# A four-layer graph network on one core: the last 68 gathered groups of the fourth layer summed from the gather's buffers, and a bias moved to GpSimd

## The reference

```python
# first layer: an MLP on each node's features and its summed edge features
agg = segment_sum(edge_attr, senders, N)
h = relu(concatenate([agg, nodes], axis=1) @ W1 + b1)      # 256 -> 512
return h @ W2 + b2                                         # 512 -> 128: b2 is the bias that moves

# second and third layer: sums of neighbours' rows x[src], dense matrices (no part of the change)

# fourth layer: attention with three heads; row2, col2 are the edges' starts and ends
a_src = einsum('nhc,hc->nh', (x @ W).reshape(n, 3, 128), att_src)     # a_dst alike
alpha = leaky_relu(a_src[row2] + a_dst[col2] + a_edge)
m = segment_max(alpha, col2, n)
ex = exp(alpha - m[col2])
attn = ex / segment_sum(ex, col2, n)[col2]
agg = segment_sum(attn[:, :, None] * xp[row2], col2, n)
y = (agg.reshape(n, 384) + gat_bias) @ lin_W + lin_b
```

## Time and profile before

| | us |
|---|---|
| median of 3 runs (lowest, highest) | 3746.25 (3742.75, 3749.92) |
| the profiled execution, its own time | 3734.14 |
| its span, first to last instruction | 3732.5 |
| PE busy over the span | 2576.2 (69%) |
| DVE busy | 1566.4 (42%) |
| POOL busy | 1376.2 (37%) |
| ACT busy | 705.3 (19%) |
| mean granted clock of PE | 0.768 |

### The profile page before, as it was taken

The page is one execution under the profiler, slowest core; times in us unless marked ns, Lnnn a source line. Parts: engine busy times, 40 slices in busy tenths (PEclk is TensorE's granted clock), DMA queues, the critical chain, the costliest instruction groups (busy, mean ns, idle before and its releaser), DMA issues. The chain is left out here.

```text
span 3732.5 us, 72094 instructions
## 1 busy us (share of the span) xinstructions
PE 2576.2 (69%) x21824; PEld 2171.2 (58%) x21825; DVE 1566.4 (42%) x3762; ACT 705.3 (19%) x1093; POOL 1376.2 (37%) x1473
## 2 busy tenths in 40 slices
PE   1699999897999459996998155545550156566675
PEld 0566666784888348885887144444440156565564
DVE  5466666123111631112333455554568233233367
ACT  0287777252000410001000000000000100000033
POOL 4222222111000212221444655555530566666545
PEclk9899999897999669998999555555565555555577
DMA  4388888423887178886998555555540466666621
GB/s 119 106 282 280 283 283 283 145 58 119 283 282 248 50 221 251 247 250 194 290 291 244 139 126 124 130 131 123 128 99 13 129 171 180 170 177 173 172 67 42
DMA packets 597630, 662.89 MB, mean 178 GB/s; under 512 B 268059, under 2 KB 449388, under 8 KB 596905
## 3 DMA queue, kind: packets, MB, share of 16 engines
q1 hardware_dynamic: 276921, 405.43, 35.2%
q10 hardware_dynamic: 270440, 182.02, 17.5%
q0 software_dynamic: 50208, 74.70, 8.3%
HBM read 502.38 MB, written 159.93 MB: 177 GB/s over the span
## 5 line engine op out<-in xcount | busy, mean ns | idle before, releaser
L866 POOL DMA_INDIRECT rows<-x_rows,src_i x832 | 813.9, 978 | 663.7 <-issue 228.4
L1500 PE MATMUL ps<-slices,wide 128*128 128x250 f16 x7350 | 829.0, 271 | 55.8 <-DVE wide L2168 34.1
L1500 PEld LDWEIGHTS ps<-slices,wide 128*128 128x128 f16 x7350 | 716.3, 98 | 143.9 <-DVE wide L2168 50.3
L1450 PE MATMUL ps<-weighted,slices 128*128 128x57 f32 x1664 | 386.8, 421 | 324.8 <-issue 155.6
L1726 PE MATMUL ps<-slices 128*128 128x75 bf16 x4992 | 366.8, 249 | 332.1 <-issue 288.8
L1450 PEld LDWEIGHTS ps<-weighted,slices 128*128 128x128 f32 x1664 | 365.1, 329 | 346.4 <-issue 201.0
L1726 PEld LDWEIGHTS ps<-slices 128*128 x4992 | 309.4, 130 | 389.4 <-issue 387.7
L906 POOL TENSOR_TENSOR ea_one<-ea,ones 128x64 f32<-128x64 f32 x250 | 137.3, 550 | 454.5 <-DMA ea<-in_edge_attr 435.0
L1395 PE MATMUL ps<-rows,weighted 128*32 128x128 f32 x2000 | 272.1, 280 | 14.4 <-DMA ea<-in_edge_attr 11.8
L1395 PEld LDWEIGHTS ps<-rows,weighted 128*32 128x32 f32 x2000 | 202.4, 111 | 59.5 <-issue 51.5
L2468 DVE TENSOR_TENSOR hT<-ps,hT 128x600 f32<-128x600 f32 x104 | 81.1, 781 | 326.3 <-remote 161.9
(11 more groups left out here) (354 smaller groups left out, 3356.7 us busy)
## 6 DMA issues: line engine op xcount, KB each, us to landing
slices<-adjacency SPq DMA_DIRECT2D x525, 437.5 KB, 4.4
rows<-in_edge_attr SPq DMA_DIRECT2D x250, 256.0 KB
x_of_edges<-rows SPq DMA_DIRECT2D x208, 256.0 KB
slices<-x_of_edges ACTq DMA_DIRECT2D x208, 256.0 KB
adjacency<-wide ACTq DMA_DIRECT2D x91, 437.5 KB, 3.1
adjacency<-slices ACTq DMA_DIRECT2D x84, 437.5 KB, 3.1
slices<-src_low ACTq DMA_DIRECT2D x52, 512.0 KB
rows<-x_rows,src_i POOLq DMA_INDIRECT x832
```

The costliest lines, as they stand in the source:

```text
L866: pool.indirect_dma_start(out=packed[i][:, c, :], out_offset=None, in_=table, in_offset=bass.IndirectOffsetOnAxis(ap=rows_of, axis=0)).the ...
L1450: mm = pe.matmul(ps_a[i][:, width * h:width * (h + 1)], rows3[i][:, n, :], weighted[:, i, n, :, :].rearrange("p h w -> p (h w)"), start=(c ...
L1500: mm = pe.matmul(ps_d[b], high_low[:, part, QS * s + q, :], slices[:, s, PN * q:PN * (q + 1)], start=(s == 0 and q == 0 and part == 0), st ...
```

## The change

In the fourth layer the last 68 groups (FRESH; groups 140 to 207) are neither stored nor loaded back: PE multiplies straight from `packed`, the gather's own buffers. The first 140 (STORED) go the old way. The order of summing changes: four stored groups, then 17 rounds of 12 positions; each third position of a round is a fresh group, so that a round takes 8 stored and 4 fresh ones. PE's loop has 12 groups a turn instead of 4, DVE's too, ACT's too. Offsets are loaded to registers 8, and then 16 + 8 a round. POOL waits for scoring passes up to g = 113 instead of 103, no more for `scan_done`, and no more for a number of summed groups ahead of group 144; from there it waits until the fresh group four before has been summed. SP's loop of stores has 35 turns of four in place of 52.

In the first layer the fifth matmul of each tile goes, two in a pair. The bias is loaded to all 125 partitions, POOL adds it in place to the residual rows xb when they have landed, one pair ahead of its stores, and DVE waits for that (`x_shifted`) where it waited for the load.

```diff
-                if g >= RING:
+                if RING <= g < STORED + RING:
                     pool.wait_ge(xe_stored[i], 16 * (g // RING))
-                if SCORES_LEAD <= g < SCANNED_AT:
+                if g >= STORED + RING:
+                    pool.wait_ge(group_summed, SUMMED + place(0, 3 * (g - RING - STORED) + 2) + 1)
+                if SCORES_LEAD <= g < SCORES_LEAD + PASSES:
                     pool.wait_ge(scores_begun, g - SCORES_LEAD + 1)
-                if g == SCANNED_AT:
-                    pool.wait_ge(scan_done, 1)
-                if g >= SCANNED_AT + SUMS_LEAD:
-                    pool.wait_ge(group_summed, SUMMED + 2 * (g - SCANNED_AT - SUMS_LEAD) + 1)
...
+            def refill(u, last):                                        # ACT
+                for j in range(MIX):
...
+                    act.wait_ge(group_summed, SUMMED + place(u, j) + 1)
+                    if not is_fresh(j) and not (last and n >= RING):
+                        load_stored(RING + 2 * RING * u + n + RING, 2 + 2 * u + n // RING, n % RING)
+                    load_att(summed_group(u, j + RING), j % RING)
...
+                with pe.Fori(0, MIXED) as u:                            # PE
+                    for j in range(MIX):
+                        n = stored_at(j)
+                        if is_fresh(j):
+                            group(place(u, j), j % RING, packed[j // 3], fetched(j // 3, u))
+                        else:
+                            group(place(u, j), j % RING, rows3[n % RING], arrived(n % RING, 1 + 2 * u + n // RING))
...
-                with v.Fori(0, NIT // 2 - 1) as k:                      # DVE
-                    two_iterations(k, False)
+                def mixed(u, last):
+                    stored = bases_of(regs[0:2 * AH], RING + 2 * RING * u, 2 * RING)
+                    fresh = bases_of(regs[2 * AH:3 * AH], STORED + RING * u, RING)
+                    for j in range(MIX):
+                        p = place(u, j)
+                        if not (last and j + LEAD >= MIX):
+                            make(summed_group(u, j + LEAD), (j + LEAD) % RING)
+                        if not (last and j + 2 >= MIX):
+                            weights(p + 2, 1 + 3 * u + (j + 2) // RING, (j + 2) % RING)
+                        add(p, j % RING, fresh[j // 3] if is_fresh(j) else stored[stored_at(j)])
...
+            def biased0(q, u, s):                                       # POOL, first layer
+
+                pool.wait_ge(*d0.landed(s, u))
+                pool.tensor_tensor(xb[:, s, :, :], xb[:, s, :, :], row2[:, 0, :].unsqueeze(1).to_broadcast([TN, TP, P]),
+                                   ALU.add).then_inc(x_shifted, 1)
+
+            def rows0(q, u, s, first):
+
+                if not is_last(q):
+                    biased0(q + 1, u + s, 1 - s)
+                pool.wait_ge(d0.done, q + 1)
+                pool.dma_start(tiles_of(x1_d, q), yb[:, s:s + 1, :, 0:P]).then_inc(pair_stored[s], 16)
...
                     for m in range(H0):                                 # PE, first layer
-                        pe.matmul(..., start=(m == 0), stop=False)
-                    mm = pe.matmul(ps_y[s][:, k, :], ones[0:1, 0:TN], row2[0:1, 0, :], start=False, stop=True)
+                        mm = pe.matmul(..., start=(m == 0), stop=(m == H0 - 1))
...
                 v.wait_ge(d0.Y, q + 1)                                  # DVE, first layer
-                v.wait_ge(*d0.landed(s, u))
+                v.wait_ge(x_shifted, q + 1)
```

More of the change, by code:

```diff
@@ L469, in arrived, with fetched, is_fresh, stored_at @@
             return rows_loaded[i], 32 * len(range(i, NLW, RING)) + 16 * (u + 1)
+        def fetched(i, u):
+            return rows_landed[i], 16 * CH * (STORED // RING + u + 1)
+        def is_fresh(j):
+            return j % 3 == 2
+        def stored_at(j):
+            return 2 * (j // 3) + j % 3
+        def summed_group(u, j):
+            u, j = u + j // MIX, j % MIX
+            return STORED + RING * u + j // 3 if is_fresh(j) else RING + 2 * RING * u + stored_at(j)
+        def group_at(p):
+            return p if p < RING else summed_group(0, p - RING)
+        def place(u, j):
+            return RING + MIX * u + j
         STEPS2B = 8
@@ L1782, in _ @@
             v.reg_mov(norms, 0)
-            regs = [v.alloc_register(f"dve_base{n}") for n in range(2 * AH)]
+            regs = [v.alloc_register(f"dve_base{n}") for n in range(3 * AH)]
             meta_f = meta[:, :, :].rearrange("a n k -> a (n k)")
@@ L2073, in two_iterations, with add @@
-                def two_iterations(k, last):
-                    v.reg_load(regs, meta_f[0:1, bass.ds(2 * AH * k, 2 * AH)])
-                    bases = [v.snap(r, min_val=0, max_val=N - 1) for r in regs]
-                    for n in range(2):
-                        iteration(2 * k + n, bases[AH * n:AH * (n + 1)], last and n == 1)
-                with v.Fori(0, NIT // 2 - 1) as k:
-                    two_iterations(k, False)
-                two_iterations(NIT // 2 - 1, True)
+                def add(p, i, bases):
+                    v.wait_ge(group_summed, SUMMED + p + 1)
+                    for h in range(HALF):
+                        at = bass.ds(bases[h], W)
+                        v.wait_ge(psum_free, FREED + HALF * p + h)
+                        acc = wide[:, :, at]
+                        part = ps_a[i][:, HEADS * W * h:HEADS * W * (h + 1)].rearrange("p (h w) -> p h w", w=W)
+                        v.tensor_tensor(acc, acc, part, ALU.add).then_inc(psum_free, 1)
@@ new lines, in bases_of @@
+                def bases_of(to, g, n):
+                    v.reg_load(to, meta_f[0:1, bass.ds(HALF * g, HALF * n)])
+                    at = [v.snap(r, min_val=0, max_val=N - 1) for r in to]
+                    return [at[HALF * i:HALF * (i + 1)] for i in range(n)]
+                for p in range(LEAD):
+                    make(group_at(p), p)
+                for p in range(2):
+                    weights(p, 0, p)
+                v.wait_ge(scan_act, 2 + HEADS)
+                bases = bases_of(regs[0:AH], 0, RING)
@@ new lines, in sums @@
+                for p in range(RING):
+                    make(group_at(p + LEAD), (p + LEAD) % RING)
+                    weights(p + 2, (p + 2) // RING, (p + 2) % RING)
+                    add(p, p, bases[p])
+                def mixed(u, last):
[8 more added lines that the diff above has]
+                        add(p, j % RING, fresh[j // 3] if is_fresh(j) else stored[stored_at(j)])
@@ L2082, in sums @@
+                with v.Fori(0, MIXED - 1) as u:
+                    mixed(u, False)
+                mixed(MIXED - 1, True)
                 v.wait_ge(psum_free, FREED + NH)
```

88 lines of the change are left out of this document (43 added, 45 removed).

## The result

The changed kernel takes 3572.82 us (median of 3 runs, 3569.88 to 3575.01) against 3746.25: 173 us less, ratio 0.9536 with a 95% interval of 0.9515 to 0.9558. The profiled execution took 3569.88 us, its span is 3568.3. The prediction said 3680, 66 us less: the direction and the range (3550 to 3754) held, the size did not.

What follows compares the result with a forecast made beforehand. PE bounds the first layer; in scoring and sums each gathered group takes about 2.9 us from the loops beside it. -20 + 30 + 4 - 80 = -66 gives 3668 profiled, 3680 on the median; range 3550 to 3754.

Steps and rivals of the forecast that it cites:

- The first layer: Bias matmuls leave PE's full queue, 0.81 us a pair over 25 pairs: -20 us, ends -10 and -21.
- The cover for the addition on POOL: First layer: the bias additions, 18 us on POOL, fit in its 33 of 40 us free, ahead of the store.
- Scoring: Attention scores: ten more groups gathered beside the last five iterations, 3.0 us each: +30 us.
- The scans: Gather now runs during the scans, which don't lose; +4 us for three long transfers sharing the DMA engines.
- The rival of held scans: Scans suffer from the gather like the loops, +72 us in place of +4: 3752, no change; chance 0.12.
- The sums: Summing of groups: gathered groups beside it fall from 98 to 70, 2.84 us each: -80 us, 639 becomes 559.
- its sum for the gather: Sums: four chunks take 5.0 us, three positions at least 5.2, so the gather is no limit.
- A crawl for 25 us instead of 48: Start of the sums: sign of being right, the first additions crawl for 25 us instead of 48.
- The offsets' loads: Sums: 35 loads by DVE instead of 26, mostly under PE's backlog; at most +10 us, taken as nothing.
- Deeper buffers pay: Sums: the excess belongs to the round of four load buffers, 12.9 us, now covering six positions: 3551; chance 0.18.
- positions at 2.1 us or less: Sums: sign that the forecast is wrong and buffers are the cause; the forecast expected 2.6 to 2.8 us a position.
- The attention's ring takes over: Sums: attention values' four buffers over four positions set the 12.9 us round, sums stay 639: 3760, slower; chance 0.13.

Runs made afterwards that it cites:

- r1_after: The changed kernel itself, run again in another session: 3552.27 us against 3716.86 for the kernel before, ratio 0.9563.
- r6_weights_first: The changed kernel with DVE's offset loads put behind the first one-hot and weights of a round: 3544.97 us against 3713.63 for the kernel before, ratio 0.9533.
- k7_bias_pace3: Kernel before plus bias on GpSimd and new gather waits (one gathered group per three summed from group 141), no fresh groups: 3613.19 us against 3752.38, ratio 0.9625.
- k5: Kernel before with only gather waits changed, two paces per stage (sums: one gathered group per three summed, then per two): 3685.73 us against 3724.22, single runs.
- e2_pace2: Kernel before with only gather waits changed, one gathered group per two summed from group 144, all stored and loaded back: ratios 0.9997 and 0.9992, lower level only.

## Why the prediction was wrong

*The first layer* (-20 forecast, -27 measured). The mechanism was right, the term was mis-sized and came out past its own end of -21: it counted the slots of the removed products and not that their neighbours would close up (1.10 us a pair, not 0.81). The cover for the addition on POOL held.

*Scoring* (+30, +33.5). Right, with some luck in the size: three other profiles with these waits of the scoring (r1_after, r6_weights_first, k7_bias_pace3) have 700.6, 712.9 and 692.5 us for the stage, where this one has 696.2. In k5 a gathered group that leaves the scoring gave back 3.0 us.

*The scans* (+4, +1.1). Right. From the last score to the first addition POOL issued 89 chunks (forecast 95), 72 groups were left (forecast 70), and the scans lost no more than 1.1 us. The rival of held scans falls.

*The sums* (-80, -168.9). This is the step that failed: "The work of the sums itself stays: 208 groups x 1.72. So the stage loses 28 x 2.84 = 80 us." How many groups move was right: 98 became 72. What failed is the price: the 2.84 us were taken as fixed, also for the groups that stay, although their pace changed from one in two positions to one in three. The 2.84 is no cost of a gathered group by itself. It is what is left of the group's period when PE's work in it is taken off, and the row for the period was at hand: 595 us for 98 groups is 6.07 us each; with 184 / 98 = 1.88 positions of 1.72 us in each, 3.23 us, 2.84 are left. The change fits three positions, 5.16 us of work, into a period of 6.25, and only 1.09 are left. (Between the slow start and the last chunk, where the old kernel too is steady, a period of 6.08 holds two positions, 3.44 us, and leaves 2.64.) At the old pace the prediction's sum would have been about right: e2_pace2's expectation, by period, comes to the same 558 us of sums. POOL's window of before between the slow start and its last chunk has 90 groups:

```profile
2986.00:3533.00 547.00, 343.20 (x360) 0.50 0.63 174
```

| | slow start | gathered groups x period | after the last chunk | sum |
|---|---|---|---|---|
| before | 48 | 90 x 6.08 = 547 | 43 | 638 |
| after | 49 | 64 x 6.25 = 400 | 20 | 469 |

The differences show what was left out. The 26 groups that went from between the slow start and the last chunk give 26 x (6.08 - 3.44) = 69 us, which is the forecast's 28 x 2.84 = 80 by another count. The 64 that stayed give 64 x (2.64 - 1.09) = 99 us, for which the forecast had nothing. Together it is 168 of the 168.9. The split is worked out from these rows; the old pace with the new number of groups (pace 2) never met the upper level.

The prediction saw the pace ("one group in three positions instead of two" is in its sum for the gather) and used it only to show that the gather was no limit. k5 and k7 show that it was the pace: the same loads, stores and buffers give 2.19 to 2.23 us a position at one for three and 2.99 at one for two. The period itself is not quite fixed: 6.0 and 6.1 us at one for two, 6.6 to 7.0 at one for three through the load buffers, 6.25 with the fresh groups.

*The slow start.* "A crawl for 25 us instead of 48" failed: 49 us. In the four profiles at hand it lasts as long as POOL runs without a pause and some 9 us more, and in the first profile that was 41 us of the sums. In r1_after it was 20 us, near the forecast, with POOL further ahead.

*The offsets' loads.* They did stop PE, 3.9 us a round, which the forecast took as nothing because they would stand under PE's backlog. It was nothing all the same, but for another reason: the period covers it (r6).

*Deeper buffers pay* (3551, given 0.18) came 22 us from the time, and the prediction's own sign for it, "positions at 2.1 us or less", came true at 2.08. That sign could not tell buffers from pace, a rival that the prediction did not have. Its mechanism is refuted as the main cause: with four row buffers and four attention buffers k7 did four positions in 8.9 us, where the rival said 12.9. What buffers and saved transfers give is about 0.47 us a period, 30 us. *The attention's ring takes over* falls with 2.08 us a position, through the same four attention buffers.

*What stays open.* Why a run of gathers delays what one engine hands to another on the upper level and not on the lower one, why it did not do so in the scans, and what sets the level. The chip alone does not: chip 10 gave 3357.62, 3338.18 and 3752.38 for the kernel before.

## What to carry to other kernels

When two engines run in lockstep, count periods, not excesses: ask what one period of the partner lasts and how much of your own work your waits allow inside it. A pacing wait is then a dial of its own; try it alone before moving buffers. And an engine that issues a long series without a pause may be what holds up the others. A stretch in which all others show x0 is a place to look, but ask first which of them had work left, and see whether the series really stops where they go on.

## What the runs showed of the hardware

On the upper level engines got on late beside a series of indirect transfers on POOL (one each 1.25 us): DVE's last pick of the scores came 77 us after PE's last product (k5), and an addition 15 us late at the start of the sums. In the sums POOL was let go 1.36 to 1.45 us after the last of four chunks (the changed kernel's timeline above), and 8.6 to 10.5 us after the last of a long series. In the scans beside the same series PE and DVE took turns in 0.47 us (k5). On the lower level the series cost the scoring nothing that shows (7.5 us an iteration, which is what the upper level has without gathers). The two levels lie 11% apart for the same kernel, and the change is worth 4.5% on one and about nothing on the other.
